# A recommendation tower: eight of 432 table gathers moved from GpSimd to SyncE, one row per DMA, and the work around them reordered

## The chip, the cores and the metric

The kernel runs on one core of a Trainium2 chip, alone. The metric is device time in microseconds (us), the median of several executions. TensorE (PE), VectorE (DVE), ScalarE (ACT), GpSimd (POOL) and SyncE (SP) each run their own program in order and meet at semaphores.

## What is computed

For 2048 samples, 27 features of 128 floats each are looked up in 27 tables by `ids`. All pairs of the 27 vectors of a sample are multiplied (351 dot products), and vectors, products and 16 context values run through three layers:

```python
e = jnp.stack([tbl_0[ids[:, 0]], ..., tbl_26[ids[:, 26]]], axis=1)      # 2048 x 27 x 128
interactions = jnp.einsum('bfd,bgd->bfg', e, e)[:, triu_i, triu_j]      # 2048 x 351
h = jnp.concatenate([e.reshape(2048, -1), interactions, dense_ctx], axis=1)
h = jnp.maximum(h @ W_top1 + b_top1, 0.0)                               # 3823 -> 512
h = jnp.maximum(h @ W_top2 + b_top2, 0.0)                               # 512 -> 256
y = h @ W_top3                                                          # 256 -> 1
```

## The kernel before

The batch is cut into 16 tiles of 128 samples. Nothing is scheduled by a tool: each engine's program is written out by hand, and semaphores hold them together.

**GpSimd** fetches. For each tile it issues 27 indirect DMAs (L242), one per feature, each 128 rows of 512 bytes into `emb`. `emb` holds one tile only. The features form seven groups of four (the last has three), and the gathers of group g of the next tile wait until TensorE has transposed group g of this one (`s_pe_t`).

**TensorE** runs, per tile t: `turn_group(t, g)` (L269, four transposes into one of two banks of `ps_t`), after ACT and DVE have split the transposed group into a high and a low part `multiply(t, f)` (L298 to L300, three matmuls 128x512 per feature into `ps_acc`), and 16 `gram_unit`s (L323, two matmuls each) that make the pair products in three banks of `ps_gram`. Between them stands the rest of the tile before: `turn_columns` (L352) and `multiply_columns` (L356) for products and context, `turn_h1` (L393), and `layer_2` (L400). `BEFORE_UNIT` says how many features are multiplied ahead of each unit. Groups 0 and 1 of the next tile are turned after units 8 and 14.

**ScalarE** writes the high part (L534), **VectorE** the low part (L645). They take the units' results out of `ps_gram` alternately, four copies a unit (`take_blocks`, ACT even units L582, DVE odd units L666). A unit can start when the unit three before it has been taken. VectorE then turns the blocks (`turn_blocks`, L680), adds parts (L687), packs 351 columns (`pack_pairs`, L702) and does `layer_3` (L714, L717). ScalarE moves the transposed columns (L550, L551), applies the first relu (`relu_h1`, L565) and copies its transpose (`take_h1`, L571).

**SyncE** loads ids and weights. In tile 0 the weights of the first layer come in 27 chunks through a ring of six (L187) and are split by ACT and DVE. When all groups of tile 0 are turned, it issues ten more loads (L202 to L216), and then only waits to store the output. The last tile has an order of its own, with `gram_pair` (L345) in place of the units; the change doesn't touch that order.

Of the kernel before, what the change touches and what calls it, by code (L numbers as in the profile page):

```python
# [5 lines left out]
def dlrm_tower_kernel(nc, dense_ctx, ids, tables, w_top1, b_top1, w_top2, b_top2, w_top3, out):  # L6
# [42 lines left out]
    PAIRS = UNITS // 2  # L49

    POOL_FROM = 16
    HALF = H1 // 2

    ctx = ExitStack()
    with ctx:
# [15 lines left out]

        emb_x = sb("emb_x", [P, 2, P, Q], fp32r)
        emb = sb("emb", [P, NF * D])
        g_buf = sb("g_buf", [P, 2 * Q * XW])
        gram = sb("gram", [P, NF, NF])
        cols = sb("cols", [P, NCOL])
# [30 lines left out]
        s_w_late = sem("s_w_late")  # L107
        s_gather = [sem(f"s_gather{g}") for g in range(NG)]
        s_gather_last = sem("s_gather_last")
        s_zero = sem("s_zero")  # L110
        s_ident = sem("s_ident")
        s_pads = sem("s_pads")
# [23 lines left out]
        s_h2 = sem("s_h2")  # L136
        s_y = sem("s_y")
        s_stored = sem("s_stored")

        def emb_part(part, f):  # L140
            return emb_x[:, part, :, f]
# [39 lines left out]
        @block.sync  # L181
        def _(sp):
            def load_weights(c):
                s = c % STAGES
                if c >= STAGES:
                    sp.wait_ge(s_w_lo, c - STAGES + 1)
                sp.dma_start(stage[:, s, :], w_top1[c * P:(c + 1) * P, :]).then_inc(s_w_raw[s], 16)  # L187

            sp.dma_start(idx_first[:, :], ids.rearrange("(p t) f -> p t f", t=TILES)[:, 0, :]
                         ).then_inc(s_ids_first, 16)
            sp.wait_ge(s_ids_first, 16)
            for c in range(NF):
                load_weights(c)
                if c == GROUPS[0][-1]:
                    sp.dma_start(idx[:, :, :].rearrange("p t f -> p (t f)"),
                                 ids.rearrange("(p t) f -> p (t f)", t=TILES)).then_inc(s_ids, 16)


            sp.wait_ge(s_pe_t, NG)
            sp.dma_start(w_cols[:, 0:FULL, :], w_top1[NF * D:(NF + FULL) * D, :].rearrange(  # L202
                "(c p) n -> p c n", p=P)).then_inc(s_w_late, 16)
            sp.dma_start(w_cols[0:REST - 1, FULL, :], w_top1[(NF + FULL) * D:K1, :]
                         ).then_inc(s_w_late, 16)
            sp.dma_start(w_cols[REST - 1:REST, FULL, :], b_top1.rearrange("(o n) -> o n", o=1)
                         ).then_inc(s_w_late, 16)
            sp.dma_start(w_2[:, :, :], w_top2.rearrange("(k p) n -> p k n", p=P)
                         ).then_inc(s_w_late, 16)

            rows = dense_ctx.rearrange("(q j t) c -> j q (t c)", j=NJ, t=TILES)
            for j in range(NJ):
                sp.dma_start(ctx_rows[j * Q:(j + 1) * Q, :, :].rearrange("p t c -> p (t c)"),
                             rows[j, :, :]).then_inc(s_ctx, 16)
            sp.dma_start(b2_rows[:, :], b_top2.partition_broadcast(P)).then_inc(s_const, 16)
            sp.dma_start(w3_rows[:, :],  # L216
                         w_top3.rearrange("k o -> (k o)").partition_broadcast(P)
                         ).then_inc(s_const, 16)
            sp.wait_ge(s_y, TILES)
            sp.dma_start(out.rearrange("(p t) o -> p (t o)", t=TILES),  # L220
                         y[:, :]).then_inc(s_stored, 16)
            sp.wait_ge(s_stored, 16)

        @block.gpsimd
        def _(pool):
# [5 lines left out]
            for t in range(TILES):  # L231
                if t == 1:
                    pool.wait_ge(s_ids, 16)
                for g in range(NG):
                    if t > 0:
                        pool.wait_ge(s_pe_t, NG * (t - 1) + g + 1)
                    for f in GROUPS[g]:
                        landed = s_gather[g]
                        if t == TILES - 1 and f == NF - 1:
                            landed = s_gather_last  # L240
                        rows = idx_first[:, f:f + 1] if t == 0 else idx[:, t, f:f + 1]
                        pool.indirect_dma_start(  # L242
                            out=emb[:, f * D:(f + 1) * D], out_offset=None, in_=tables[f],
                            in_offset=bass.IndirectOffsetOnAxis(ap=rows, axis=0)
                        ).then_inc(landed, 16)
# [16 lines left out]
        def _(pe):  # L262
            def turn_group(t, g):
                n = NG * t + g
                pe.wait_ge(s_gather[g], (t + 1) * 16 * len(GROUPS[g]))
                if n >= 2:
                    pe.wait_ge(s_emb_lo, n - 1)
                for i, f in enumerate(GROUPS[g]):
                    last = pe.transpose(turned_bank(n, g)[:, :, i], emb[:, f * D:(f + 1) * D],  # L269
                                        ident[:, :])  # L270
                last.then_inc(s_pe_t, 1)

            def turn_last_group(t):

                g, n = NG - 1, NG * t + NG - 1
                pe.wait_ge(s_gather[g], 16 * ((t + 1) * len(GROUPS[g]) - 1))
                pe.wait_ge(s_emb_lo, n - 1)
                for i, f in enumerate(GROUPS[g][:-1]):
                    last = pe.transpose(turned_bank(n, g)[:, :, i], emb[:, f * D:(f + 1) * D],
                                        ident[:, :])  # L280
                last.then_inc(s_pe_t, 1)

# [157 lines left out]

            BEFORE_UNIT = [2, 0, 0, 2, 0, 0, 1, 0, 0, 1, 0, 0, 1, 0, 0, 0]
            assert len(BEFORE_UNIT) == UNITS and sum(BEFORE_UNIT) <= NF - 4 * GF

            pe.wait_ge(s_ident, 1)
# [2 lines left out]
            for t in range(TILES - 1):  # L449
                multiply_group(t, 0)  # L450
                turn_group(t, 2)
                multiply_group(t, 1)
                turn_group(t, 3)
                multiply_group(t, 2)
                if t > 0:
                    turn_columns(t - 1)
                turn_group(t, 4)
                if t > 0:
                    multiply_columns(t - 1)
                multiply_group(t, 3)  # L460
                turn_group(t, 5)
                if t > 0:
                    turn_h1(t - 1)
                f = 4 * GF
                for _ in range(GF if t == 0 else 2):
                    multiply(t, f)
                    f += 1
                turn_group(t, 6)
                for k in range(UNITS):
                    for _ in range(min(BEFORE_UNIT[k], NF - f)):  # L470
                        multiply(t, f)
                        f += 1
                    gram_unit(t, k)
                    if k in (8, 14):
                        turn_group(t + 1, (k - 8) // 6)
                if t > 0:
                    layer_2(t - 1)
                while f < NF:
                    multiply(t, f)
                    f += 1  # L480
# [41 lines left out]
        def _(act):  # L522
# [83 lines left out]
            for t in range(TILES - 1):  # L606
                for g in range(NG):
                    if t == 0:
                        for c in GROUPS[g]:
                            split_weights(c)  # L610
                    split_group(t, g)
                    if t > 0 and g == 3:
                        take_columns(t - 1)
                    if t > 0 and g == 4:
                        relu_h1(t - 1)
                    if t > 0 and g == 5:
                        take_h1(t - 1)
                for k in range(0, UNITS, 2):
                    take_blocks(t, k)
            t = TILES - 1  # L620
            for g in range(5):
                split_group(t, g)
# [12 lines left out]
        def _(dve):  # L635
# [99 lines left out]
            for t in range(TILES - 1):  # L735
                for g in range(NG):
                    if t == 0:
                        for c in GROUPS[g]:
                            split_weights(c)
                    split_group(t, g)  # L740
                    if t > 0:
                        if g == 0:
                            turn_blocks(t - 1)
                        if g == 1:
                            add_parts(t - 1)
                            pack_pairs(t - 1, 0, 10)
                        if g == 2:
                            pack_pairs(t - 1, 10, NF - 1)
                            if t > 1:
                                layer_3(t - 2)  # L750
                for k in range(1, UNITS, 2):
                    take_blocks(t, k)
            t = TILES - 1
            split_group(t, 0)
            split_group(t, 1)
            turn_blocks(t - 1)
            split_group(t, 2)
            layer_3(t - 2)
# [40 lines left out]
```

## Time and profile before

| | before |
|---|---|
| timed runs, us | 576.74 median (576.59, 576.74, 579.01) |
| span of the profiled execution, us | 708.0 |
| another time of the profiled execution | none is given |
| TensorE busy, of the span | 574.9 us, 81% |
| GpSimd busy | 416.2 us, 59% |
| VectorE busy | 347.6 us, 49% |
| ScalarE busy | 232.3 us, 33% |
| gathers by GpSimd | 27 + 405 |
| mean granted TensorE clock | 0.908 |

The profiled execution is 131.3 us longer than the median of the timed runs, so a duration of one instruction can be read from it, but the span can't be taken for the time. TensorE's busy time is modelled and overlaps from one matmul to the next; the distance between starts is the better measure.

### The profile page before, as it was taken

The numbers are of one execution on the slowest core, as the hardware profiler recorded it, in microseconds if no ns is written. First come the engines' busy times: TensorE is split into PE (matmuls) and PEld (weight loads), VectorE is DVE, ScalarE is ACT, GpSimd is POOL, SyncE is SP. The second block draws the span as 40 slices with busy tenths as digits, with TensorE's granted clock in tenths as the row PEclk, the third lists the DMA queues.
The fourth block names the chain that finished last, engine by engine and source line by source line (L and its number), as shares of the span: only waits on it lengthen the run. The fifth ranks groups of instructions, "written<-read, shape, count | busy, mean of one in ns | idle before, by whom it ended". The sixth has DMA issues, their size and how long they took to land.

```text
span 708.0 us, 7882 instructions
## 1 busy us (share of the span) xinstructions
PE 574.9 (81%) x2578; PEld 504.6 (71%) x2578; DVE 347.6 (49%) x1140; ACT 232.3 (33%) x703; POOL 416.2 (59%) x450
## 2 busy tenths in 40 slices
PE   2606688989889898959959896897968979698898
PEld 1505577868778787948848795786857868697786
DVE  4305462819264563808337281554707355372755
ACT  4204423324251513315232331514315161323441
POOL 6775565666666565665746667365664666556001
PEclk9956899989989998989989899799987999989999
DMA  6613411111111111111111111011110111111000
GB/s 211 217 52 110 131 45 44 46 46 44 45 45 50 41 49 41 48 45 39 47 29 50 44 42 52 27 49 42 46 52 26 49 41 49 42 41 46 12 1 1
DMA packets 19581, 37.84 MB, mean 53 GB/s; under 512 B 7780, under 2 KB 8804, under 8 KB 19540
## 3 DMA queue, kind: packets, MB, share of 16 engines
q0 software_dynamic: 13824, 28.34, 15.1%
q1 hardware_dynamic: 5716, 8.99, 4.0%
q8 instruction: 21, 0.34, 0.2%
q14 instruction: 20, 0.16, 0.1%
HBM read 37.30 MB, written 0.01 MB: 53 GB/s over the span
## 4 chain that ended last, share of the span: by engine, by line
PE 59%; another core or an unknown queue 20%; DVE 8%; issue 6%; ACT 5%; DMA 1%; SPq 0%; ACTq 0%; DVEq 0%
PE ps_acc L298 12%; PE ps_acc L299 11%; PE ps_acc L300 11%; PE ps_gram L323 10%; DVE g_buf L666 6%; PE ps_acc L356 6%; PE ps_t L269 5%; PE ps_gram L400 3%; ACT g_buf L582 2%; DVE emb_x L645 1%; DMA g_buf<-in_W_top 1%; ACT emb_x L534 1%; ACT h_t L571 1%; PE ps_gram L352 1%
## 5 line engine op out<-in xcount | busy, mean ns | idle before, releaser
L242 POOL DMA_INDIRECT emb<-in_tbl,idx x405 | 385.8, 953 | 233.4 <-issue 109.4
L298 PE MATMUL ps_acc<-w_hi,emb_x 128*128 128x512 f32 x432 | 211.1, 489 | 28.7 <-DVE emb_x L645 26.6
L645 DVE TENSOR_TENSOR emb_x<-ps_t,emb_x 128x512 fp32r<-128x512 f32 (+1 forms) x111 | 73.9, 667 | 249.6 <-ACT emb_x L534 165.2
L299 PE MATMUL ps_acc<-w_lo,emb_x 128*128 128x512 f32 x432 | 182.7, 423 | 0.0
L300 PE MATMUL ps_acc<-w_hi,emb_x 128*128 128x512 f32 x432 | 181.0, 419 | 0.0
L666 DVE COPY g_buf<-ps_gram 32x112 f32<-32x112 f32 x480 | 129.8, 270 | 93.6 <-PE ps_gram L323 63.1
L323 PE MATMUL ps_gram<-emb_x 128*128 128x224 f32 x480 | 99.5, 335 | 79.2 <-DVE emb_x L645 41.2
L298 PEld LDWEIGHTS ps_acc<-w_hi,emb_x 128*128 128x128 f32 x432 | 131.9, 305 | 35.3 <-DVE emb_x L645 28.0
L323 PEld LDWEIGHTS ps_gram<-emb_x 128*128 128x128 f32 x480 | 83.4, 231 | 102.0 <-DVE emb_x L645 45.1
L582 ACT ACTIVATE g_buf<-ps_gram 32x112 f32<-32x112 f32 x480 | 122.2, 255 | 99.0 <-PE ps_gram L323 64.8
L534 ACT ACTIVATE emb_x<-ps_t 128x512 fp32r<-128x512 f32 (+1 forms) x111 | 63.1, 583 | 272.7 <-PE ps_t L269 137.4
L299 PEld LDWEIGHTS ps_acc<-w_lo,emb_x 128*128 128x128 f32 x432 | 134.4, 311 | 3.9
L300 PEld LDWEIGHTS ps_acc<-w_hi,emb_x 128*128 128x128 f32 x432 | 132.6, 307 | 4.2
L269 PE MATMUL ps_t<-ident,emb 128*128 128x128 f32 x429 | 68.7, 284 | 17.5 <-DMA emb<-in_tbl,idx_first 17.1
L269 PEld LDWEIGHTS ps_t<-ident,emb 128*128 128x128 f32 x429 | 53.8, 146 | 24.6 <-issue 13.2
L680 DVE STREAM_TRANSPOSE g_buf<-g_buf 128x1792 f32<-128x1792 f32 x16 | 59.2, 3697 | 0.1
L356 PE MATMUL ps_acc<-w_cols,cols_t 128*128 128x512 f32 (+1 forms) x96 | 45.5, 609 | 4.7 <-issue 3.8
L702 DVE TENSOR_TENSOR cols<-gram,g_buf 128x26 f32<-128x26 f32 (+25 forms) x406 | 39.0, 174 | 0.0
L356 PEld LDWEIGHTS ps_acc<-w_cols,cols_t 128*128 128x128 f32 (+1 forms) x96 | 17.0, 190 | 23.3 <-issue 20.8
L242 POOL DMA_INDIRECT emb<-in_tbl,idx_first x27 | 26.9, 996 | 9.2 <-issue 7.9
L400 PE MATMUL ps_gram<-w,h_t 128*128 128x256 f32 x112 | 27.0, 385 | 0.0
L400 PEld LDWEIGHTS ps_gram<-w,h_t 128*128 128x128 f32 x112 | 20.7, 195 | 2.3
(61 smaller groups left out, 163.2 us busy)
## 6 DMA issues: line engine op xcount, KB each, us to landing
g_buf<-in_W_top SPq DMA_DIRECT2D x27, 256.0 KB
emb<-in_tbl,idx POOLq DMA_INDIRECT x405
w_cols<-in_W_top SPq DMA_DIRECT2D x1, 512.0 KB
w<-in_W_top SPq DMA_DIRECT2D x1, 512.0 KB
emb<-in_tbl,idx_first POOLq DMA_INDIRECT x27
w_cols<-in_W_top SPq DMA_DIRECT2D x1, 222.0 KB
idx<-in_ids SPq DMA_DIRECT2D x1, 216.0 KB, 4.9
ctx_rows<-in_dense_ctx SPq DMA_DIRECT2D x4, 32.0 KB
```

What stands on the lines that cost most here:

```text
L242: pool.indirect_dma_start(out=emb[:, f * D:(f + 1) * D], out_offset=None, in_=tables[f], in_offset=bass.IndirectOffsetOnAxis(ap=rows, axis ...
L269: last = pe.transpose(turned_bank(n, g)[:, :, i], emb[:, f * D:(f + 1) * D], ident[:, :])
L298: pe.matmul(acc, emb_part(0, f), w_hi[:, f, :], start=(f == 0), stop=False)
L299: pe.matmul(acc, emb_part(0, f), w_lo[:, f, :], start=False, stop=False)
L300: last = pe.matmul(acc, emb_part(1, f), w_hi[:, f, :], start=False, stop=False)
L323: last = pe.matmul(ps_gram[:, n % BANKS, i * NJ * XW:(i + 1) * NJ * XW], gram_weights(q), gram_stream(q), start=True, stop=True)
L356: return pe.matmul(ps_acc[:, t % 2, :], cols_t[0:k, n * P:(n + 1) * P], w_cols[0:k, n, :], start=False, stop=(n == NCC - 1))
L400: last = pe.matmul(ps_late[:, 0:H2], h1_t[:, k * P:(k + 1) * P], w_2[:, k, :], start=(k == 0), stop=(k == K2 - 1))
L534: act.activation(group_part(0, g), turned_bank(n, g), ACT.Copy).then_inc(s_emb_hi, 1)
L582: last = act.activation(target, source, ACT.Copy)
L645: dve.tensor_tensor(group_part(1, g), turned_bank(n, g), group_part(0, g).bitcast(fp32), ALU.subtract).then_inc(s_emb_lo, 1)
L666: last = dve.tensor_copy(target, source)
```

## The change

SyncE fetches feature 23 (`AHEAD`, in group 5) of the eight tiles 3, 5, 7, 9, 11, 13, 14 and 15, into a buffer of its own for each, `ahead`. It first loads the 8 x 128 ids side by side into `idx_ahead`, then takes 16 of them at a time into its registers and issues one DMA of 512 bytes per row, 1,024 in all. GpSimd skips these eight gathers. `turn_group(t, 5)` waits for all 128 rows (`s_ahead`), and reads them from `ahead`.

With it the tiles 0 to 14 get another order. On TensorE, `turn_columns` moves behind `multiply_group(t, 3)`, `multiply_columns` behind two features of group 4, `turn_h1` behind unit 8, and the units have nine features ahead of them instead of seven. ScalarE does `relu_h1` after the split of group 6, and `take_h1` after its take of unit 8. VectorE splits group 0 of the next tile before it takes unit 15, and group 1 before it turns the blocks.

```diff
+    AHEAD = 23
+    AHEAD_TILES = [3, 5, 7, 9, 11, 13, 14, 15]
+    NA = len(AHEAD_TILES)
+    LOAD = 16
...
+        ahead = sb("ahead", [P, NA, D])
+        idx_ahead = sb("idx_ahead", [NA, P], i32)
...
+        def fetched_ahead(t, f):
+            return f == AHEAD and t in AHEAD_TILES
...
+                for n, t in enumerate(AHEAD_TILES):
+                    sp.dma_start(idx_ahead[n:n + 1, :], ids.rearrange(
+                        "(p t) f -> t f p", t=TILES)[t, AHEAD:AHEAD + 1, :]
+                        ).then_inc(s_ids_ahead, 16)
+            sp.wait_ge(s_ids_ahead, 16 * NA)
+            for n in range(NA):
+                for p in range(0, P, LOAD):
+                    _, picked = nc.values_load_multi_w_load_instructions(
+                        idx_ahead[n:n + 1, p:p + LOAD], engines=[mybir.EngineType.SP],
...
+                    for i in range(LOAD):
+                        sp.dma_start(ahead[p + i:p + i + 1, n, :],
+                                     tables[AHEAD][bass.ds(picked[i], 1), :]
+                                     ).then_inc(s_ahead[n], 16)
             sp.wait_ge(s_y, TILES)
...
                     for f in GROUPS[g]:
+                        if fetched_ahead(t, f):
+                            continue
...
-                pe.wait_ge(s_gather[g], (t + 1) * 16 * len(GROUPS[g]))
+                pe.wait_ge(s_gather[g], gathered(t, g))
+                if AHEAD in GROUPS[g] and t in AHEAD_TILES:
+                    pe.wait_ge(s_ahead[AHEAD_TILES.index(t)], 16 * P)
...
-            BEFORE_UNIT = [2, 0, 0, 2, 0, 0, 1, 0, 0, 1, 0, 0, 1, 0, 0, 0]
+            BEFORE_UNIT = [2, 0, 0, 2, 0, 0, 2, 0, 0, 1, 0, 0, 2, 0, 0, 0]
...
                 multiply_group(t, 2)
+                turn_group(t, 4)
+                multiply_group(t, 3)
                 if t > 0:
                     turn_columns(t - 1)
-                turn_group(t, 4)
-                if t > 0:
-                    multiply_columns(t - 1)
-                multiply_group(t, 3)
                 turn_group(t, 5)
-                if t > 0:
-                    turn_h1(t - 1)
                 f = 4 * GF
                 for _ in range(GF if t == 0 else 2):
                     multiply(t, f)
                     f += 1
+                if t > 0:
+                    multiply_columns(t - 1)
                 turn_group(t, 6)
...
                     gram_unit(t, k)
+                    if k == 8 and t > 0:
+                        turn_h1(t - 1)
...
-                    split_group(t, g)
+                    if t == 0 or g > 1:
+                        split_group(t, g)
...
                 for k in range(1, UNITS, 2):
+                    if k == UNITS - 1:
+                        split_group(t + 1, 0)
                     take_blocks(t, k)
+                split_group(t + 1, 1)
```

The order of VectorE's instructions from the units of one tile on, before (L666 is the take of a unit, L645 the split, L680 `turn_blocks`, L687 `add_parts`, L698 and L702 `pack_pairs`):

```order
L666 COPY g_buf<-ps_gram 32x112 x32
L645 TENSOR_TENSOR emb_x<-ps_t,emb_x 128x128x4
L680 STREAM_TRANSPOSE g_buf<-g_buf 128x1792
L645 TENSOR_TENSOR emb_x<-ps_t,emb_x 128x128x4
L687 TENSOR_TENSOR gram<-g_buf 128x729
L698 COPY cols<-ctx_rows 128x16
```

The same place after the change (L709 is the take, L688 the split, L723 `turn_blocks`, L730 `add_parts`):

```order
L709 COPY g_buf<-ps_gram 32x112 x28
L688 TENSOR_TENSOR emb_x<-ps_t,emb_x 128x128x4
L709 COPY g_buf<-ps_gram 32x112 x4
L688 TENSOR_TENSOR emb_x<-ps_t,emb_x 128x128x4
L723 STREAM_TRANSPOSE g_buf<-g_buf 128x1792
L688 TENSOR_TENSOR emb_x<-ps_t,emb_x 128x128x4
L730 TENSOR_TENSOR gram<-g_buf 128x729
```

Two splits now stand ahead of `turn_blocks`, the first of them ahead of the last take.

The order of SyncE after the change, from its last old load on (L244 loads ids, L250 puts 16 of them in registers, L255 is one row's address arithmetic and its DMA; the pair of L255 stands 16 times behind each L250, and L250 64 times in all; before the change nothing stands between `w_rows` and the store of `y`):

```order
L239 DMA w_rows<-in_W_top 128x256
L244 DMA idx_ahead<-in_ids 1x128x1 x8
L250 TENSOR_LOAD idx_ahead
L255 ISA
L255 DMA ahead<-in_tbl 1x128
L255 ISA
L255 DMA ahead<-in_tbl 1x128
```

Each row costs SyncE an arithmetic instruction and a DMA of one partition.

## Rows read from the trace of the kernel before

**Rows 1.** The page: span, TensorE's busy time, the chain by engine.

```profile
span 708.0 us, 7882 instructions
...
PE 574.9 (81%) x2578; PEld 504.6 (71%) x2578; DVE 347.6 (49%) x1140; ACT 232.3 (33%) x703; POOL 416.2 (59%) x450
...
PE 59%; another core or an unknown queue 20%; DVE 8%; issue 6%; ACT 5%; DMA 1%; SPq 0%; ACTq 0%; DVEq 0%
```

**Rows 2.** Who waited for whom: us in total, times, longest.

```profile
ACT emb_x L534 <- remote: 106.9, 16, 27.5
POOL emb L242 <- PE ps_t L269: 94.0, 35, 9.3
...
PE ps_gram L323 <- DVE g_buf L666: 13.5, 25, 3.8
...
PE ps_gram L323 <- ACT g_buf L582: 11.6, 12, 2.1
```

**Rows 3.** The chain that ended last, tile 0: start, us, what.

```profile
28.19 27.46 another core or an unknown queue
...
70.11 0.23 PE ps_acc L299
...
71.29 1.01 PE ps_gram L323 x6
```

**Rows 4.** Timeline of GpSimd: first, two neighbouring and last gather (start, us).

```profile
2.78 1.14 POOL L242 DMA_INDIRECT emb<-in_tbl,idx_first  x1 [1.30 <-DMA idx_first<-in_ids]
...
196.97 0.94 POOL L242 DMA_INDIRECT emb<-in_tbl,idx  x1 [0.30 <-issue]
198.22 0.95 POOL L242 DMA_INDIRECT emb<-in_tbl,idx  x1 [0.30 <-issue]
...
655.83 0.94 POOL L242 DMA_INDIRECT emb<-in_tbl,idx  x1 [0.30 <-issue]
```

**Rows 5.** Timeline of TensorE and ScalarE, end of tile 3's first part.

```profile
186.49 0.60 PE L269 MATMUL ps_t<-ident,emb 128*128 128x128 f32 x4
...
191.75 0.60 ACT L534 ACTIVATE emb_x<-ps_t 128x512 fp32r<-128x512 f32 x1 [7.28 <-remote]
...
193.86 1.11 PE L323 MATMUL ps_gram<-emb_x 128*128 128x224 f32 x6 [2.98 <-DVE emb_x L645]
```

**Rows 6.** By stretch: tile 2's units, then units' end to tile 3's.

```profile
154.50:167.00 12.50, 11.85 (x55) 10.44 (x56) 7.43 (x28) 7.51 (x30) 8.20 (x10) 0.77 0.16 42
167.00:193.90 26.90, 23.71 (x109) 21.24 (x107) 13.34 (x44) 6.01 (x14) 17.44 (x19) 1.00 0.18 47
```

**Rows 7.** Timeline of SyncE's queue: DMAs issued (start, us).

```profile
0.75 0.38 SPq L191 DMA_DIRECT2D idx_first<-in_ids  x1
2.52 1.75 SPq L187 DMA_DIRECT2D g_buf<-in_W_top  x4
...
69.79 0.38 SPq L202 DMA_DIRECT2D w_cols<-in_W_top  x1
...
70.66 0.28 SPq L206 DMA_DIRECT2D w_cols<-in_b_top  x1
70.97 0.40 SPq L208 DMA_DIRECT2D w<-in_W_top  x1
...
73.94 0.43 SPq L216 DMA_DIRECT2D w_rows<-in_W_top  x1
```

**Rows 8.** Timeline of TensorE, last tile: groups 5 and 6 turned.

```profile
681.07 0.60 PE L269 MATMUL ps_t<-ident,emb 128*128 128x128 f32 x4
...
683.47 0.38 PE L279 MATMUL ps_t<-ident,emb 128*128 128x128 f32 x2
```

**Rows 9.** The chain that ended last, tile 14's units begin.

```profile
650.22 0.94 PE ps_gram L323 x6
```

**Rows 10.** VectorE: groups by line, mean ns; one `turn_blocks` in the timeline.

```profile
L666 DVE COPY g_buf<-ps_gram 32x112 f32<-32x112 f32 x480 | 129.8, 270 | 93.6 <-PE ps_gram L323 63.1 <-remote 19.0 <-issue 4.0
...
210.14 3.71 DVE L680 STREAM_TRANSPOSE g_buf<-g_buf 128x1792 f32<-128x1792 f32 x1
```

More of the change, by code:

```diff
@@ L109, in dlrm_tower_kernel @@
         s_gather_last = sem("s_gather_last")
+        s_ids_ahead = sem("s_ids_ahead")
+        s_ahead = [sem(f"s_ahead{t}") for t in AHEAD_TILES]
         s_zero = sem("s_zero")
@@ L138, in dlrm_tower_kernel, with rows_of, gathered @@
         s_stored = sem("s_stored")
+        def fetched_ahead(t, f):
+            return f == AHEAD and t in AHEAD_TILES
+        def rows_of(t, f):
+            if fetched_ahead(t, f):
+                return ahead[:, AHEAD_TILES.index(t), :]
+            return emb[:, f * D:(f + 1) * D]
+        def gathered(t, g):
+            return 16 * sum(1 for u in range(t + 1) for f in GROUPS[g] if not fetched_ahead(u, f))
         def emb_part(part, f):
@@ L218, in _ @@
                          ).then_inc(s_const, 16)
+            with nc.allow_non_contiguous_dma(reason="one id of every row of ids"):
+                for n, t in enumerate(AHEAD_TILES):
[7 more added lines that the diff above has]
+                        idx_ahead[n:n + 1, p:p + LOAD], engines=[mybir.EngineType.SP],
+                        min_val=0, max_val=tables[AHEAD].shape[0] - 1,
+                        skip_runtime_bounds_check_because="an id is a row of its table")
+                    for i in range(LOAD):
+                        sp.dma_start(ahead[p + i:p + i + 1, n, :],
+                                     tables[AHEAD][bass.ds(picked[i], 1), :]
+                                     ).then_inc(s_ahead[n], 16)
             sp.wait_ge(s_y, TILES)
@@ L237, in _ @@
                     for f in GROUPS[g]:
+                        if fetched_ahead(t, f):
+                            continue
                         landed = s_gather[g]
@@ L268, in turn_group @@
                 for i, f in enumerate(GROUPS[g]):
-                    last = pe.transpose(turned_bank(n, g)[:, :, i], emb[:, f * D:(f + 1) * D],
+                    last = pe.transpose(turned_bank(n, g)[:, :, i], rows_of(t, f),
                                         ident[:, :])
@@ L278, in turn_last_group @@
                 for i, f in enumerate(GROUPS[g][:-1]):
-                    last = pe.transpose(turned_bank(n, g)[:, :, i], emb[:, f * D:(f + 1) * D],
+                    last = pe.transpose(turned_bank(n, g)[:, :, i], rows_of(t, f),
                                         ident[:, :])
@@ L611, in _ @@
                     split_group(t, g)
-                    if t > 0 and g == 3:
+                    if t > 0 and g == 4:
                         take_columns(t - 1)
-                    if t > 0 and g == 4:
+                    if t > 0 and g == 6:
                         relu_h1(t - 1)
-                    if t > 0 and g == 5:
-                        take_h1(t - 1)
                 for k in range(0, UNITS, 2):
                     take_blocks(t, k)
+                    if t > 0 and k == 8:
+                        take_h1(t - 1)
             t = TILES - 1
@@ L739, in _ @@
                             split_weights(c)
-                    split_group(t, g)
+                    if t == 0 or g > 1:
+                        split_group(t, g)
                     if t > 0:
-                        if g == 0:
+                        if g == 1:
                             turn_blocks(t - 1)
-                        if g == 1:
+                        if g == 2:
                             add_parts(t - 1)
                             pack_pairs(t - 1, 0, 10)
-                        if g == 2:
+                        if g == 3:
                             pack_pairs(t - 1, 10, NF - 1)
@@ L751, in _ @@
                 for k in range(1, UNITS, 2):
+                    if k == UNITS - 1:
+                        split_group(t + 1, 0)
                     take_blocks(t, k)
+                split_group(t + 1, 1)
             t = TILES - 1
-            split_group(t, 0)
-            split_group(t, 1)
             turn_blocks(t - 1)
```

## Prediction

> **What bounds the kernel now.** I read the chain on the page first: PE holds 59% of it, and 20%, 141.6 us of 708.0, stands under "another core or an unknown queue" [rows 1]. The waits say what that is: 16 waits of ScalarE for transposes, 106.9 us, whose end the profile can't name [rows 2]. The longest is 27.46 us in tile 0 [rows 3]. One from tile 3 in detail: TensorE's record has the group's transposes begin at 186.49, but ScalarE is let go at 191.75, and TensorE then idles 2.98 us for the split before the units [rows 5]. The timed runs take 576.74 us, 131.3 less than the span, about the size of these waits. I choose to take them as absent from the timed runs: then the sum has to be made against 576.74, with durations of single instructions from the trace.
>
> Without them, two engines come out nearly equal.
>
> *GpSimd.* Two neighbouring gathers start 1.25 us apart, 0.95 of it busy [rows 4]; 27 make 33.7 us per tile. In the profiled execution GpSimd still waits 94.0 us for TensorE [rows 2], because there each tile takes 39 to 44 us. With no wait at all, the first gather at 2.78 and 432 x 1.25 = 540 us end at 542.8, and from the last feature's transposes to the end are 708.0 - 683.5 = 24.5 us [rows 4, 8]: a floor of 567.3 us plus one landing.
>
> *TensorE.* From the last unit of a tile to the next tile's first are 26.9 us, 3.0 of them the idle above: 23.9. The units take 12.5 us at a mean granted clock of 0.77 [rows 5, 6]. That mean is 2.9 us lost to the lower level (1.2 instead of 2.4 GHz), where TensorE was the limit; about half of it can come back, since the copies pace the rest. VectorE's eight takes of four copies at 0.27 to 0.28 give 9 us [rows 10]. So units are 9.5 to 11, and a tile 33.4 to 34.9.
>
> *The timed run's own tile.* Tile 0's units begin at 71.3, less 22.6 of the long wait (27.46 without the 5 us that work beside it fills, my estimate): 48.7. From tile 14's units to the end are 708.0 - 650.2 = 57.8 [rows 3, 9]. That leaves (576.7 - 48.7 - 57.8) / 14 = 33.6 us per tile, at GpSimd's 33.7 and TensorE's lower end. Neither alone is worth much; the change lightens both.
>
> **The change part by part.**
>
> *Eight gathers off GpSimd.* 8 x 1.25 = 10.0 us [rows 4]. Its floor goes to 557.3 plus the landing, its mean tile to 33.1. Nothing on that path takes their place.
>
> *TensorE's order.* Two more features stand ahead of units, and `turn_h1` among them: 6 x 0.24 + 0.44, near 1.9 us a tile that leave the stretch without copies for the one that the copies pace [rows 3, 6]. What they can fill there are TensorE's waits for the takes, 13.5 + 11.6 = 25.1 us in 15 tiles, 1.7 each [rows 2]. Some of these lie where a multiply can't reach (units 1, 2, 4, 5), so from 0 to 1.7; I take 0.8, the middle, which over 14 tiles is 11 us. TensorE alone would then end at 566, GpSimd alone near 559. I let the later one decide and stay with 10.7 off: 566.
>
> *VectorE's order.* Two splits of 0.7 us precede `turn_blocks` (3.71 us), and the first also holds up the last take, since it waits for ScalarE's split, and that for ScalarE's last take. The packed columns come 2 to 2.5 us later. `turn_columns` moves behind a group of multiplies (12 x 0.24 = 2.9) and a `turn_group` (0.44), so this is covered, by about 1 us, and costs 0. Were the cover gone, it would cost up to 2.5 x 14 = 35 us. In return groups 0 and 1 are split before TensorE asks for them; before, the second stood behind the 3.71 us [rows 10], covered by the 2.9 of group 0. I count 0.
>
> *ScalarE's.* `relu_h1` and `take_h1` (0.60 each) move into places where ScalarE waits anyway: in the two stretches it is busy 7.51 of 12.5 and 6.01 of 26.9 us [rows 6]. 0.
>
> *SyncE.* It has been idle since its last load. In the timed runs `w_cols` is issued at 69.8 - 22.6 = 47.2, the last at 51.8 [rows 7]. Eight id loads at 0.31 (a DMA of one partition) to 0.5 are 4 us, their landing 1.8 as for `idx_first` (0.75 to 2.52) [rows 7]: the first row goes out at 57.2 or so. The last tile's group 5 is transposed 708.0 - 681.1 = 26.9 us before the end [rows 8], at 539.1 in my forecast. So 1,024 rows have 539.1 - 57.2 - 1.8 = 480 us: **0.469 us a row** is the most that SyncE may take. The earlier tiles ask less (tile 14: 896 rows by 506, 0.50; tile 13: 0.54; tile 3: 128 rows by 141, 0.65).
>
> What it takes the trace shows in part only. The nearest row is the DMA of `b_top1`, one partition and one run: 0.28 us, the next starts 0.31 later [rows 7]. That is the lower bound. To it come the address arithmetic (no row here), the address from a register (no row), and a sixteenth of a register load. For the load the landing of `idx_first` gives 1.8/16 = 0.11 as an upper end; a whole further gap like GpSimd's between indirect DMAs, 0.30 [rows 4], I take as the upper bound of all three together: 0.31 to 0.61. I take 0.44, nearer the low end, because the row's transfer is the same in kind as `b_top1`'s and register arithmetic moves no data. Then the rows are in at 57.2 + 451 + 1.8 = 510, 29 us early, and cost nothing.
>
> On the register load the Trainium skill has a figure, in "DMA: Bandwidth & Descriptors", section "Latency and other measured facts": a floor of about 600 ns for `tensor_load`. No row here shows it. By it a sixteenth is an estimated 0.04 us, and the row 0.35 plus the arithmetic.
>
> **The rivals.**
>
> 1. *SyncE too slow* (0.20). It ends on the other side. From the threshold on every row is on the path: time = 57.2 + 1024 r + 1.8 + 26.9 = 85.9 + 1024 r. At r = 0.479 nothing is left of the gain, at 0.50 it is 598, at 0.61 710. For it: two instructions a row, neither seen in this trace. Against: the 0.31 of `b_top1`, and 0.16 of room above it.
>
> 2. *TensorE stays the bound* (0.11). If the units are paced by the copies and the 1.9 us go in at their full length, the tile stays at 33.6 and time at 574 to 578. For it: the takes alone make 9 us of 9.5 to 11. Against: 25.1 us of named waits that work can fill.
>
> 3. *The columns come late* (0.04). VectorE's chain outgrows the 3.3 us of cover: 1 us late is 14 us, 580; the decisive point is about 1.0 us of further delay.
>
> 4. *One row at a time* (0.03). If a row's DMA had to land before the next could start, each would take the 1.4 us from the end of `idx_first`'s issue (0.75 + 0.38) to the next engine's start at 2.52: 86 + 1024 x 1.4 = 1,520 us. Against: the weight loads of tile 0, issued 0.44 us apart [rows 7], didn't wait for each other's landing. The Trainium skill speaks for this case: "DMA: Bandwidth & Descriptors", section "Why a DMA increments its semaphore by 16 and not by 1", has the engines of a DMA from SyncE chosen by its slowest dimension, so that a transfer of one partition may use a single one, and the semaphore written only after that engine's data. All 1,024 rows would share one of 16 engines. The rows here don't show which engine a transfer used.
>
> **How the numbers follow.** The forecast (both engines lightened, SyncE in time) has 0.62: 566 us, 555 to 573 by the 0 to 1.7 of TensorE's waits and GpSimd's floor with its landing. The range of all cases reaches on the slow side to 600, SyncE at 0.502 a row; beyond lie half of rival 1 and rival 4, some 0.14 together, and below 555 perhaps 0.03. What a measurement can tell from no change is 0.5%, 573.9 to 579.6. Faster: 0.62 and 0.02 of rival 1 (r under 0.476); same: most of rival 2 and 0.02 of rival 1, 0.12; slower: the rest, 0.24.
>
> **What would show each step right or wrong.** In the new profile GpSimd has 397 + 27 gathers, still 1.25 us apart. SyncE's rows follow each other within 0.40 to 0.47 us, the stretch of 1,024 ends near 510, and no wait of `turn_group(t, 5)` on `s_ahead` appears; spacing above 0.48 makes the prediction wrong, even if a profiled execution as long as 700 us hides it. TensorE's waits for the takes (L323) fall from 25.1 us to about half; if they stay, rival 2 holds. TensorE's waits ahead of the column transposes stay under 0.3 us a tile; if not, rival 3. If the unexplained waits of ScalarE are in the timed runs after all, the base of every tile time here is wrong, and the saving of GpSimd is not on the path.

## The result, and the profile after

The changed kernel takes 594.43 us (592.27 to 598.74), the kernel before 577.37 us beside it: a ratio of 1.031, interval 1.027 to 1.035. It is slower by 17 us where 566 was forecast. The profiled execution has a span of 593.5 us and took 595.35 us in all, so some 1.9 us lie around the span.

The page of the changed kernel, the lines that answer to [rows 1], with the granted clock in 40 slices between them:

```profile
span 593.5 us, 11020 instructions
...
PE 535.8 (90%) x2578; PEld 480.7 (81%) x2578; DVE 348.0 (59%) x1140; ACT 232.8 (39%) x703; POOL 411.7 (69%) x442
...
PE   0787999999999999999999999999999999994097
...
PEclk9988999999999999999999999999999999998589
...
POOL 39%; PE 36%; issue 17%; DMA 3%; ACT 3%; DVE 3%; ACTq 0%; POOLq 0%; DVEq 0%
```

TensorE is busy to nine tenths in every slice but the first four and three of the last four, which stand at 4, 0, 9 and 7. The hole at 4 and 0 is the result. Its timeline in the last tile, ahead of group 5's transposes (L312 is L269 of before; `x3` from `emb`, `x1` from `ahead`):

```profile
537.75 2.74 PE L399 MATMUL ps_acc<-w_cols,cols_t 128*128 128x512 f32 x6
564.05 0.87 PE L312 MATMUL ps_t<-ident,emb 128*128 128x128 f32 x3 [23.56 <-issue]
564.71 0.42 PE L312 MATMUL ps_t<-ident,ahead 128*128 128x128 f32 x1
```

The profile calls the 23.56 us "issue", since it finds no instruction that ended them. SyncE's stream says what did. One line of source each: count, duration min/median/max in ns, first and last start in us:

```profile
L250 SPq TENSOR_LOAD <-idx_ahead x64: 1179/1232/1406, 58.0 to 554.8; - x64
L255 SPq FUSED_REGOPS  x1024: 37/37/51, 59.2 to 562.5; - x171
L255 SPq MOVE ahead<-in_tbl x1024: 29/29/42, 59.3 to 562.5; - x171
L255 SPq DMA_DIRECT2D ahead<-in_tbl x1024: 219/220/312, 59.4 to 562.6; - x171
```

The last of 1,024 rows goes out at 562.6 and ends its issue at 562.8; TensorE goes on at 564.05, 1.45 us after the start of the last row's DMA, one landing later. From 59.4 to 562.6 are 0.492 us a row, over the 0.469 that the prediction named as the most. By stretch: a whole tile (units to units), the last 28 us before the hole, the hole, and the rest:

```profile
78.70:111.70 33.00, 32.63 (x162) 29.65 (x161) 20.78 (x71) 13.62 (x43) 25.08 (x27) 1.00 0.20 55
512.10:540.50 28.40, 27.78 (x137) 24.40 (x136) 19.45 (x69) 12.16 (x40) 21.39 (x24) 1.00 0.21 54
540.50:564.05 23.55, 0.00 (x1) 0.03 (x1) 0.00 (x0) 0.60 (x1) 0.00 (x0) 0.60 0.02 4
564.05:593.50 29.45, 26.01 (x113) 20.87 (x113) 15.31 (x43) 9.21 (x26) 2.65 (x11) 0.91 0.01 1
```

This tile takes 33.0 us. From one tile's first unit to the next one's are 33.05 to 33.13 us in nine of thirteen (tiles 2 to 14) and 33.89 to 33.99 in four, the tiles 6, 8, 10 and 12: SyncE fetches nothing for them, and in each a group's transposes wait 0.54 to 0.63 us for one of GpSimd's gathers (the tiles 2 and 4 get nothing from SyncE either, and don't wait). The mean is 33.34.

After the hole TensorE starts at its lower clock: from 564.05 to 569.20 the granted clock is 0.50 (1.2 GHz), in the 6 us behind it 1.00. The last stretch is 29.45 us long, 2.4 more than the same work in e_seven below, which has no hole (540.96 to 568.0, granted clock 1.00).

### The profile page after: what moved, and what is told of

It is laid out like the page before. It is cut to its first block, busy times and chain, and to the rows that moved or that the text cites. A ratio compares the mean times of both kernels' runs of the same rounds, so it can differ in the third digit from the quotient of the medians.

```text
span 593.5 us, 11020 instructions
## 1 busy us (share of the span) xinstructions
PE 535.8 (90%) x2578; PEld 480.7 (81%) x2578; DVE 348.0 (59%) x1140; ACT 232.8 (39%) x703; POOL 411.7 (69%) x442
## 3 DMA queue, kind: packets, MB, share of 16 engines
q1 hardware_dynamic: 8916, 9.53, 5.2%
## 4 chain that ended last, share of the span: by engine, by line
POOL 39%; PE 36%; issue 17%; DMA 3%; ACT 3%; DVE 3%; ACTq 0%; POOLq 0%; DVEq 0%
POOL emb L283 39%; PE ps_acc L341 8%; PE ps_acc L342 7%; PE ps_acc L343 7%; PE ps_acc L399 4%; PE ps_gram L366 4%; PE ps_t L312 3%; DMA emb<-in_tbl,idx 3%; ACT g_buf L625 2%; DVE emb_x L688 1%; PE ps_gram L436 1%; DVE g_buf L723 1%; ACT emb_x L577 1%; ACT g_buf L634 0%; PE ps_gram L395 0%
## 5 line engine op out<-in xcount | busy, mean ns | idle before, releaser
L283 POOL DMA_INDIRECT emb<-in_tbl,idx x397 | 381.6, 961 | 121.1 <-issue 119.2
L341 PE MATMUL ps_acc<-w_hi,emb_x 128*128 128x512 f32 x432 | 201.1, 466 | 5.4 <-DVE emb_x L688 5.4
L688 DVE TENSOR_TENSOR emb_x<-ps_t,emb_x 128x512 fp32r<-128x512 f32 (+1 forms) x111 | 74.1, 667 | 172.1 <-ACT emb_x L577 171.6
L342 PE MATMUL ps_acc<-w_lo,emb_x 128*128 128x512 f32 x432 | 174.8, 405 | 0.0
L343 PE MATMUL ps_acc<-w_hi,emb_x 128*128 128x512 f32 x432 | 173.8, 402 | 0.0
L709 DVE COPY g_buf<-ps_gram 32x112 f32<-32x112 f32 x480 | 129.7, 270 | 53.8 <-PE ps_gram L366 47.1
L312 PE MATMUL ps_t<-ident,emb 128*128 128x128 f32 x421 | 66.9, 280 | 46.7 <-issue 23.6
L312 PEld LDWEIGHTS ps_t<-ident,emb 128*128 128x128 f32 x421 | 51.6, 144 | 61.7 <-issue 45.1
L366 PEld LDWEIGHTS ps_gram<-emb_x 128*128 128x128 f32 x480 | 69.5, 190 | 11.1 <-ACT g_buf L625 3.6
L366 PE MATMUL ps_gram<-emb_x 128*128 128x224 f32 x480 | 75.8, 285 | 1.9 <-DVE g_buf L709 1.0
L723 DVE STREAM_TRANSPOSE g_buf<-g_buf 128x1792 f32<-128x1792 f32 x16 | 59.1, 3694 | 0.1
L399 PE MATMUL ps_acc<-w_cols,cols_t 128*128 128x512 f32 (+1 forms) x96 | 44.0, 593 | 0.1
```

What stands on the lines that cost most here:

```text
L283: pool.indirect_dma_start(out=emb[:, f * D:(f + 1) * D], out_offset=None, in_=tables[f], in_offset=bass.IndirectOffsetOnAxis(ap=rows, axis ...
L312: last = pe.transpose(turned_bank(n, g)[:, :, i], rows_of(t, f), ident[:, :])
L341: pe.matmul(acc, emb_part(0, f), w_hi[:, f, :], start=(f == 0), stop=False)
L342: pe.matmul(acc, emb_part(0, f), w_lo[:, f, :], start=False, stop=False)
L343: last = pe.matmul(acc, emb_part(1, f), w_hi[:, f, :], start=False, stop=False)
L366: last = pe.matmul(ps_gram[:, n % BANKS, i * NJ * XW:(i + 1) * NJ * XW], gram_weights(q), gram_stream(q), start=True, stop=True)
```

## Experiments

**The kernel before, profiled again.**

> The kernel before, unchanged, profiled once more. If the long unexplained waits of ScalarE belong to that one profiled execution alone, the span is now 575 to 577 us, with GpSimd's gathers back to back (waits for TensorE under 10 us in place of 94) and a tile of about 33.6 us. If they belong to the kernel, they appear again, and the span is near 700.

The page and the waits of this second profile:

```profile
span 575.0 us, 7882 instructions
...
PE 534.1 (93%) x2578; PEld 479.9 (83%) x2578; DVE 347.8 (60%) x1140; ACT 232.2 (40%) x703; POOL 416.6 (72%) x450
...
PE 77%; DVE 11%; POOL 5%; issue 3%; ACT 2%; DMA 1%; ACTq 0%; POOLq 0%; DVEq 0%
```

```profile
ACT emb_x L534 <- PE ps_t L269: 188.0, 65, 5.1
DVE emb_x L645 <- ACT emb_x L534: 159.4, 52, 5.6
POOL emb L242 <- issue: 131.0, 430, 0.3
...
PEld ps_gram L323 <- DVE g_buf L666: 25.2, 58, 0.6
```

The "remote" waits of [rows 2] and GpSimd's 94.0 us for TensorE are gone, and the span agrees with the timed 576.8 us: the profile shown before the prediction was of a disturbed execution (what disturbed it isn't known). The base that the prediction chose, 576.74 and no such waits, was the right one. A tile of this kernel, units and the rest:

```profile
79.00:89.20 10.20, 9.30 (x56) 8.36 (x56) 7.37 (x28) 7.49 (x30) 7.76 (x9) 1.00 0.19 55
89.20:113.00 23.80, 23.60 (x110) 21.44 (x109) 13.44 (x44) 6.15 (x14) 18.01 (x20) 1.00 0.18 51
```

Together 34.0 us, TensorE busy throughout; from 60 to 530 us no transpose waits for a gather, and GpSimd waits for TensorE once, 0.3 us. Its last gather starts at 546.19, so 431 steps of 1.261 us from 2.75 on: 34.0 us a tile. TensorE's tiles, first unit to first unit, are 33.93 each. Both engines have the same tile to within what can be read.

**The order alone, the fetch without its last tile, and the fetch alone.** The changed kernel with

```diff
-    AHEAD_TILES = [3, 5, 7, 9, 11, 13, 14, 15]
+    AHEAD_TILES = []                               # e_order
+    AHEAD_TILES = [3, 5, 7, 9, 11, 13, 14]         # e_seven
```

> The new order alone: no tile is fetched by SyncE, GpSimd issues all 432 gathers. Theory S (SyncE's rate is the whole loss): GpSimd is the bound, eight gathers more than in the changed kernel move its end from 540 to 550 us, with 1.8 for the landing, 25.2 for the tail and 1.9 around the span 575 to 579, no different from before. Theory O (the new order costs time by itself): over 585.

> The change without tile 15: seven tiles fetched by SyncE, 896 rows. Theory S: the rows are in at 58 + 896 x 0.492 = 499 us, before tile 14's group 5 is asked for (about 504), and the 23.6 us wait of the last tile is gone: 569 to 572. Theory O: only the one gather changes, the time stays over 585.

and, as e_fetch, the changed kernel with `BEFORE_UNIT` and the loops of TensorE, ScalarE and VectorE as they were before:

> The fetch alone, eight tiles, with the order of before on TensorE, ScalarE and VectorE. Theory S: the last row is issued at 562.8 us whatever the order, so 592 to 596, the changed kernel's time. Theory O: the order of before takes the loss away, 567 to 577.

| | us, median | ratio to before, interval |
|---|---|---|
| order alone (e_order) | 574.6 | 0.997 (0.995 to 0.999) |
| order, seven tiles (e_seven) | 569.94 | 0.988 (0.985 to 0.991) |
| old order, eight tiles (e_fetch) | 593.56 | 1.028 (1.026 to 1.030) |
| order, eight tiles (the change) | 594.43 | 1.031 (1.027 to 1.035) |

The kernel before took 576.1 to 577.8 us beside the runs of this section, so differences of 1 us between rows say nothing; each ratio is to the kernel before of its own session.

The new order doesn't cost; it gains 0.3%, just below the 575 to 579 that were expected. With either order eight tiles take 594, because the last row goes out at 562.6 or 561.3 whatever the other engines do. One tile less turns a loss of 3% into a gain of 1.2%: its last row goes out at 498.1, and the transpose that reads the last of them starts at 506.7. Removing that one tile gives back 24.5 us and costs GpSimd one gather.

**The rate and the start of SyncE's stream.** All eight tiles and the new order, with

```diff
-    LOAD = 16
+    LOAD = 32        # e_load32
+    LOAD = 8         # e_load8
```

> Thirty-two ids per register load, 32 loads in place of 64, all else as in the changed kernel. If a load's 1.26 us is fixed, a row costs 0.4035 + 1.26 / 32 = 0.443 us, the last row goes out at 58 + 454 = 512 us and the 23.6 us wait is gone: 569 to 572. If a load costs by the id, the row stays at 0.49 and the time at 592 to 597.

> Eight ids per register load, 128 loads. Fixed cost of a load: 0.4035 + 1.26 / 8 = 0.561 us a row, the last row at 633, the end at 594.4 + 70 = 664 us. Cost by the id: 592 to 597.

and with the eight loads of ids moved up:

```diff
+            with nc.allow_non_contiguous_dma(reason="one id of every row of ids"):
+                for n, t in enumerate(AHEAD_TILES):
+                    sp.dma_start(idx_ahead[n:n + 1, :], ids.rearrange(
...
             sp.wait_ge(s_pe_t, NG)
```

> The eight id loads are issued before SyncE waits for tile 0, so that the first row goes out about 8 to 10 us earlier; the rate is unchanged. If SyncE's stream is the path to the end, the time falls by the same amount, microsecond for microsecond: 584 to 587. If something other than the stream holds the last tile, it stays at 592 to 597.

| | first row | last row | us a row | span | from last row to end | time, us |
|---|---|---|---|---|---|---|
| e_load8 | 57.0 | 587.0 | 0.518 | 616.9 | 29.9 | 619.36 |
| the change | 59.4 | 562.6 | 0.492 | 593.5 | 30.9 | 594.43 |
| e_fetch | 58.0 | 561.3 | 0.492 | 591.9 | 30.6 | 593.56 |
| e_early | 48.0 | 556.3 | 0.497 | 587.2 | 30.9 | 587.95 |
| e_load32 | 59.4 | 548.1 | 0.478 | 578.8 | 30.7 | 579.53 |

In five kernels between 580 and 619 us the end stands 29.9 to 30.9 us behind the last row: the stream is the path, microsecond for microsecond. Both guesses about the register load were wrong, and the truth lies between them. The loads of 8 and of 32 ids, after the one of 16 above:

```profile
L250 SPq TENSOR_LOAD <-idx_ahead x128: 690/784/947, 56.1 to 583.2; - x128
```

```profile
L250 SPq TENSOR_LOAD <-idx_ahead x32: 2029/2124/2276, 57.1 to 532.9; - x32
```

784, 1232 and 2124 ns lie on one line, 0.34 us fixed and 0.056 per id, so a larger load saves only the fixed part. e_early took 587.95 us, 6.5 less and not 8 to 10: the first row is 11.4 us earlier, but each row takes 0.005 us more (its DMA 225 ns in place of 220), 5 us in all. The DMA takes 225 ns in v_best below too, which also loads the ids early; why is open.

**Constant addresses.** This kernel leaves out the lookup of feature 23 in eight tiles; it fetches rows 0 to 127 of the table instead.

```diff
-                for p in range(0, P, LOAD):
-                    _, picked = nc.values_load_multi_w_load_instructions(
...
+                for p in range(P):
+                    sp.dma_start(ahead[p:p + 1, n, :], tables[AHEAD][p:p + 1, :]
+                                 ).then_inc(s_ahead[n], 16)
```

> This kernel leaves the lookup of feature 23 in eight tiles out: the 1,024 row DMAs have constant addresses (rows 0 to 127 of the table), no ids in registers and no address arithmetic. If the address work is what made the row cost 0.49 in place of 0.31, the rows follow each other at 0.25 to 0.31 us, all are in by 380 us, and the time is 568 to 571. If the DMA itself is paced by something else (its one engine, the landing of the one before), the spacing stays at 0.4 or more.

570.28 us, ratio 0.986 (0.982 to 0.991). Its stream of row DMAs:

```profile
L250 SPq DMA_DIRECT2D ahead<-in_tbl x1024: 214/248/345, 55.3 to 356.2; - x171
```

0.294 us a row. So 0.198 of the 0.492 are the net cost of addresses from registers. All eight tiles are in time here, so this is also the case that the prediction forecast, but for the lookup: 1.4% less than before (0.9 to 1.8), where 566 of 576.7 is 1.9%.

**Early ids and 32 at a time together (v_best).**

> All eight tiles, ids loaded early and 32 at a time. The two savings together: the first row at 48.0 us, 1,024 rows at 0.478 to 0.483, the last at 537 to 542, landed 1.2 us later, about when the last tile asks for it (540). GpSimd's last gather at 539 is then the bound: 568 to 571, one gather less than with seven tiles. If the two savings don't add up (the row 5 ns longer with early ids was only one sign), 572 to 577.

573.28 us, ratio 0.991 (0.988 to 0.995): faster than before, and outside the 568 to 571 expected. The rows take 0.483 us, the last goes out at 541.5, and the last tile still waits:

```profile
542.77 0.52 PE L312 MATMUL ps_t<-ident,emb 128*128 128x128 f32 x3 [2.92 <-issue]
```

Two savings of 6.5 and 15 us bring 21: they add up, and fall 3 us short of the need; the 572 to 577 expected for savings that don't add up was met for another reason. The wait has its price behind it too: the granted clock is 0.50 from 544.07 to 547.28. The best version found is e_seven, at 0.988; its interval and that of v_best overlap, but its last tile doesn't wait.

## Why the prediction was wrong, point by point

The time lies inside the range of all cases, 555 to 600, only because its slow side was kept for rival 1; the forecast case, 566 with 555 to 573, did not come.

**What bounds the kernel: right.** TensorE and GpSimd nearly equal, at 33.6 and 33.7 us a tile in the prediction, 33.9 and 34.0 in the second profile. The 33.6 came from two ends that were both too long: tile 0's units begin at 41.9 there and not at 48.7, and from tile 14's units to the end are 54.8 us and not 57.8.

**Eight gathers off GpSimd: the mechanism right, the size a little less.** 8 x 1.25 = 10.0 us were forecast. The last gather starts at 546.2 with 432 of them, in both orders, and at 539.1 in the changed kernel: 7.2 earlier, 8.0 in e_fetch, 5.0 in e_early. The gathers' mean rose, first e_order, then the changed kernel:

```profile
L284 POOL DMA_INDIRECT emb<-in_tbl,idx x405 | 385.8, 952 | 123.4 <-issue 121.0 <-PE ps_t L313 2.4
```

```profile
L283 POOL DMA_INDIRECT emb<-in_tbl,idx x397 | 381.6, 961 | 121.1 <-issue 119.2
```

The 9 ns are some 3 us over the kernel. The median is 944 ns in both, so a few long gathers make the difference. The row DMAs alone don't explain it: with the old order and such a stream of rows the mean is 952 (e_fetch7) and 955 (e_fetch). What lengthens some gathers stays open.

**TensorE's order: right, the size in part by luck.** 33.6 to 32.8 was forecast; measured are 33.93 before and 33.05 to 33.13 in the tiles that don't wait for a gather, 33.34 in the mean. So the two bounds take turns: taking the later of the two engines, as the prediction did, leaves out that in four tiles GpSimd holds the other one up. Its units and the rest, to be held against the two lines of the second profile above:

```profile
78.70:89.70 11.00, 10.94 (x67) 10.33 (x66) 7.57 (x28) 8.06 (x31) 8.26 (x10) 1.00 0.20 54
89.70:111.70 22.00, 21.70 (x98) 19.32 (x97) 13.21 (x43) 5.56 (x13) 16.82 (x18) 1.00 0.20 56
```

The rest is 1.8 us shorter and the units 0.8 longer, though two features and `turn_h1` more stand in them. The waits for the takes, 25.1 in [rows 2], are 13.0 in the matmuls of the second profile of before and 1.0 here:

```profile
PE ps_gram L323 <- DVE g_buf L666: 13.0, 29, 0.4
```

```profile
PE ps_gram L366 <- DVE g_buf L709: 1.0, 2, 0.6
```

The moved work fills nearly all of them, not half. The 0.8 us a tile was the middle of 0 to 1.7, and the 1.7 came from the disturbed execution; undisturbed there were 0.9 a tile to be had, and nearly all of it came.

That each half gains little alone, as forecast of two equal bounds, shows in the pair: the order alone 0.3% (GpSimd then holds most tiles at 33.7 to 33.9). For the other half:

> Seven tiles fetched by SyncE, in time, with the order of before. If TensorE is the bound of that order (tile of 33.93 us in the second profile of before, GpSimd never waiting), seven gathers less change nothing: 575 to 578. If GpSimd is the bound there, 7 x 1.25 us less: 567 to 569.

It took 577.77 us, 1.003 (1.002 to 1.004) of before: seven gathers less on GpSimd gained nothing while TensorE kept its tile of 33.9. Together they give 1.2%.

**VectorE's and ScalarE's order: right.** TensorE's matmuls wait once for the packed columns, 0.25 us in the last tile; rivals 3 and 2 fell.

**SyncE: the step that failed.** The deadline was sound: first row at 57.2 forecast, 59.4 measured; the last tile asks at 540.5, forecast 539.1. The price of a row was not: "I take 0.44, nearer the low end, because the row's transfer is the same in kind as `b_top1`'s and register arithmetic moves no data". Taken apart, with what each instruction took and the gaps behind it:

| part of a row | prediction, us | measured, us |
|---|---|---|
| DMA | 0.31, the lower bound | 0.27 from a register, 0.294 constant |
| address arithmetic | with the load 0.13 | 0.13: 0.037 and 0.029, each with a gap of about 0.03 |
| register load, a sixteenth | | 0.08 |
| steps that took longer, up to 0.8 us (some 80 of 1,024), spread over all rows | none | 0.01 |
| sum | 0.44 | 0.492 |

The last two rows of SyncE's stream, 0.40 us apart, are such a pair without a load between them:

```profile
562.19 0.62 SPq L255 DMA_DIRECT2D ahead<-in_tbl  x2
```

The DMA was even cheaper than `b_top1`'s row in [rows 7]; the work around it cost 0.22, not 0.13, since one line of address code became two instructions and two gaps, and a load costs 1.232 us for 16 ids. An error of 0.05 us, 12%, in the price of something done 1,024 times became 53 us on a stream with 29 us of slack. Rival 1 had the mechanism, its threshold and its slope: 85.9 + 1024 x 0.492 = 589.7. The profiled execution took 595.35: 1.9 more around the span, 2.2 in the first row's start and 2.5 in the tail with its lower clock (29.45 against 26.9), less 0.4 in the landing (1.45 against 1.8) and 0.6 by counting 1,024 steps where the stream takes 503.2 us. Its sign, a spacing above 0.48, came. Rival 1 was given 0.20; with bounds of 0.31 to 0.61 and a threshold of 0.469, in the middle of them, near a half would have been fair.

**One row at a time: fell.** In the changed kernel the rows go out every 0.492 us, and the last one has landed 1.45 us after its start; one at a time, 1,024 rows would have taken 1,485 us, not 503. So they overlap. They do so although a row wasn't spread over many DMA engines: SyncE's queue has 3,200 packets more than before (8,916 against 5,716), and with 1,024 single ids among them at most two are left for each row. On the register load the estimate from the Trainium skill ("DMA: Bandwidth & Descriptors", section "Latency and other measured facts", a floor of about 600 ns) was 0.04 us a row; measured are 1.232 us for 16, twice the floor and 0.08 a row, and the measurement decides: the floor holds for 8 ids (0.69 at the least), but each id adds 0.056.

## What to carry to other kernels

Before work is moved to an idle engine, its rate has to be held against the deadline of the last item, and the slack divided by the count is the error that the price may have: here 29 us over 1,024 rows, 0.03 us. Where no row shows an instruction, its gap counts too, and a threshold in the middle of the bounds is an even bet. A stream that runs late costs all of its lateness at its last item, so giving up one item can be worth more than making all of them faster: dropping one tile gained 24.5 us, the faster loads with early ids 21.

## What the runs showed of the hardware

A load of n ids into SyncE's registers takes 0.34 + 0.056 n us (8, 16 and 32 ids: 0.784, 1.232, 2.124). A DMA of one row of 512 bytes is issued every 0.294 us with a constant address; with its address from a register the DMA itself is shorter, 0.220 against 0.248 us median, but the row takes 0.40 with the arithmetic. GpSimd's indirect gather of 128 such rows takes 0.944 us (median) and the next starts 0.30 us later, with and without row DMAs beside it (b0, e_order, e_fetch7, the change). TensorE's granted clock was at 0.50 (1.2 GHz) from 564.05 to 569.20, right behind the wait of 23.56 us, and in v_best from 544.07 to 547.28, shortly behind one of 2.92 us.
